# The second column correction is made directly behind its sums, and VectorE adds it to x tile 4

## The reference, cut to what matters

```
def fake_quant(x, s, z):
    q = clip(round(x / s + z), 0, 255)
    return (q - z) * s

x = x + fake_quant(layernorm(x), s1, z1) @ fake_quant(ctx, s2, z2)

y = layernorm(x)
logits = y @ gate_w.T                     # 8 experts, top 2, softmax over the two
x = x + y @ base_w.T + base_b + 2 * sum_e w_e * (y @ A_e.T) @ B_e.T     # rank 16 each
```

## Time and profile before

| what | value |
|---|---|
| median of 3 runs | 197.53 us (196.81 to 198.03) |
| the profiled execution's own time | 196.73 us |
| its span, first to last instruction | 194.9 us |
| mean granted TensorE clock | 0.982 |
| PE busy | 170.9 us (88%) |
| DVE busy | 123.3 us (63%) |
| ACT busy | 77.6 us (40%) |
| POOL busy | 16.2 us (8%) |

### The profile page before, as it was taken

How to read it: one execution, slowest core, us unless ns; L and a number is a source line. 1 busy time by engine, 2 the same in 40 slices (tenths; PEclk the granted TensorE clock), 3 DMA queues, 4 the chain that set the end, 5 groups by cost and what they waited for, 6 DMA issues and landing times.

```text
span 194.9 us, 2441 instructions
## 1 busy us (share of the span) xinstructions
PE 170.9 (88%) x862; PEld 123.3 (63%) x862; DVE 123.3 (63%) x314; ACT 77.6 (40%) x132; POOL 16.2 (8%) x33
## 2 busy tenths in 40 slices
PE   5837687959898998997888399999999999999993
PEld 2312243548686877885376276878688868888882
DVE  0688566889989969899403856765675506561521
ACT  2366949809247152756550412732243230110000
POOL 2022003201010000000041100110011000100000
PEclk9996999999999999999999789999999999999999
DMA  4999996999947520322019590425053500350112
GB/s 90 403 415 409 412 408 256 199 243 347 308 182 152 174 87 20 120 100 108 0 27 182 114 219 0 94 49 148 35 100 58 166 3 0 53 162 0 59 54 105
DMA packets 9515, 29.55 MB, mean 152 GB/s; under 512 B 1184, under 2 KB 1184, under 8 KB 9504
## 3 DMA queue, kind: packets, MB, share of 16 engines
q1 hardware_dynamic: 7344, 22.06, 30.3%
q0 software_dynamic: 2016, 7.34, 20.3%
q10 hardware_dynamic: 144, 0.00, 0.0%
HBM read 22.05 MB, written 4.19 MB: 135 GB/s over the span
## 4 chain that ended last, share of the span: by engine, by line
PE 56%; DVE 23%; ACT 10%; DMA 5%; issue 5%; SPq 0%; DVEq 0%; ACTq 0%
PE ps_odd L837 17%; PE ps_even L837 16%; PE ps_att L795 6%; PE ps_g L829 3%; PE ps_t L779 3%; DMA x_sb<-zfix 2%; DMA x_sb<-in_x 2%; DVE stats L515 2%; DVE x_sb L568 2%; DVE yt L593 2%; DVE stats L511 2%; DVE c L557 2%; ACT zfix L365 1%; DVE w_lo L599 1%; ACT qx L337 1%
## 5 line engine op out<-in xcount | busy, mean ns | idle before, releaser
L837 PE MATMUL ps_even<-w_hi,yt 128*128 128x512 f32 x128 | 38.0, 403 | 0.8 <-ACT zfix L365 0.8
L837 PE MATMUL ps_odd<-w_hi,yt 128*128 128x512 f32 x128 | 36.7, 400 | 0.0
L837 PEld LDWEIGHTS ps_even<-w_hi,yt 128*128 128x128 f32 x128 | 23.7, 192 | 5.6 <-issue 1.0
L795 PE MATMUL ps_att<-c,c1t 128*128 128x512 f16 x96 | 23.9, 389 | 2.3 <-ACT c1t L344 2.3
L837 PEld LDWEIGHTS ps_odd<-w_hi,yt 128*128 128x128 f32 x128 | 22.8, 188 | 4.2
L385 ACT ACTIVATE yt<-ps_t 128x512 fp32r<-128x512 f32 x15 | 9.0, 597 | 33.2 <-PE ps_t L779 33.2
L837 PE MATMUL ps_even<-w_lo,yt 128*128 128x512 f32 x64 | 20.9, 403 | 0.0
L593 DVE TENSOR_TENSOR yt<-ps_t,yt 128x512 fp32r<-128x512 f32 x15 | 10.4, 690 | 15.1 <-ACT yt L385 14.9
L319 ACT ACTIVATE ln_v<-mv,eps 128x1 f32<-128x1 f32 x16 | 4.7, 293 | 37.8 <-DVE mv L516 37.8
L829 PE MATMUL ps_g<-ag,yt 128*128 128x272 f32 x64 | 17.2, 343 | 2.1 <-DVE yt L593 2.1
L837 PE MATMUL ps_odd<-w_lo,yt 128*128 128x512 f32 x64 | 18.7, 392 | 0.0
(11 more groups left out here) (99 smaller groups left out, 252.8 us busy)
## 6 DMA issues: line engine op xcount, KB each, us to landing
ring<-in_ctx SPq DMA_DIRECT2D x12, 512.0 KB, 10.1
w_raw<-in_w_t SPq DMA_DIRECT2D x8, 512.0 KB, 15.5
x_sb<-in_base_b POOLq DMA_DIRECT2D x8, 512.0 KB, 5.4
out_x<-x_sb SPq DMA_DIRECT2D x16, 256.0 KB, 2.5
x_sb<-in_x SPq DMA_DIRECT2D x7, 512.0 KB, 6.5
x_sb<-zfix POOLq DMA_DIRECT2D x6, 512.0 KB, 5.4
x_sb<-in_ctx SPq DMA_DIRECT2D x4, 512.0 KB, 7.9
ag_raw<-in_ag_t SPq DMA_DIRECT2D x1, 544.0 KB, 14.1
```

The source lines that it names most:

```text
L795: ins = pe.matmul(att_bank(t)[h][:, :], c1t[:, t % 4, k, :], c2[:, k, h * HALF:(h + 1) * HALF], start=(k == 0), stop=(k == CT - 1))
L837: pe.matmul(ffn_bank[t % 2][h][:, :], rows_of(part, t, k), w[:, k, h * HALF:(h + 1) * HALF], start=start, stop=False)
```

## The change: what it does

ScalarE makes the second column correction ahead of `scale_x(5)`, and so ahead of the row corrections of tiles 2 and 3 as well. GpSimd no longer issues the DMA that adds it to x tile 4. A new VectorE step `add_zfix_early` adds it, between the constants of tile 5 and `cut_x(5)`, once both halves of `zfix` and the quantisation of tile 4 are there. `add_attention(4)` waits for a semaphore of that step in place of the DMA's. Tiles 5, 6 and 7 still get the correction by DMA. On GpSimd the bias of tile 3 now stands directly behind the bias of tile 2.

```diff
-        zfix_added = {t: sem(f"zfix_added{t}") for t in range(2, TILES)}
+        zfix_added = {t: sem(f"zfix_added{t}") for t in range(2, TILES) if t != TPB}
+        x4_fixed = sem("x4_fixed")
...
@@ GpSimd
             for t in range(TPB, TILES):
-                add_zfix(t)
+                if t > TPB:
+                    add_zfix(t)
                 add_bias(t - 1)
             add_bias(TILES - 1)
@@ ScalarE
             first_guess(0, 5)
+            zero_point_columns(1)
             scale_x(5)
             zero_point_row(2)
             zero_point_row(3)
-            zero_point_columns(1)
@@ VectorE, in add_attention
                 if t == 0:
                     dve.wait_ge(ss_ready, 1)
+                elif t == TPB:
+                    dve.wait_ge(x4_fixed, 1)
                 elif t > 1:
                     dve.wait_ge(zfix_added[t], 16)
@@ VectorE
+            def add_zfix_early():
+                dve.wait_ge(zfix_ready, 4)
+                dve.wait_ge(qx_ready[TPB], 1)
+                dve.tensor_tensor(x_sb[:, TPB, :], x_sb[:, TPB, :], zfix[:, :], ALU.add).then_inc(x4_fixed, 1)
...
             sum_context(7)
             x_constants(5)
+            add_zfix_early()
             cut_x(5)
```

## The result

The changed kernel takes 189.84 us (median of 4 runs, 189.57 to 191.78). The ratio to the kernel before is 0.9636, with a 95% interval of 0.9548 to 0.9723. It is faster, by about the 3.5% that were forecast (190.7 us, range 189.2 to 193.0). The ratio compares the fast executions alone (without one of the kernel before at 200.22 us), so it is not the quotient of the medians. The profiled execution took 189.90 us with a span of 188.1 and a mean granted clock of 0.991; before it was 194.9 and 0.982, so 6.8 us of span are gone, against 6.63 in the sum.

A forecast was written before the change was run, and what follows sets the result against it. TensorE, busy 88%, bounds the kernel, with waits of 4.1 us for y and 0.8 us for zfix. Removing 5.16 us of standing still and 1.47 us of slow clock gives 190.1 us profiled; forecast 190.7 us, range 189.2 to 193.0.

The forecast's parts named there:

- the sum: Block 3 on TensorE shrinks from 25.95 to 19.32 us, a gain of 6.63 us that reaches the end.
- The path: Tile 4's chain into block 3: correction, its addition, attention, y and transposition all come earlier, y ready at 102.8.
- The stop: TensorE's standing still in block 3, waiting for zfix and y of tile 4, goes: 5.16 us.
- The margin of 2.6 us for y: Tile 4's y is ready at 102.8, 2.6 us before TensorE comes to its transposition at 105.46.
- The clock: Behind the wait for y, TensorE's stretch at half clock goes: 1.47 us.
- What was to cost nothing: Work moved on ScalarE, VectorE and the earlier bias transfer loses nothing; covers of 1.1, 0.3 and 4.7 us.
- The shared port: GpSimd's bias issue beside busy VectorE costs 0, upper bound 0.86 us; the skill's rule suggests up to half a microsecond.
- The first: Rival: TensorE's clock falls all the same, in block 3 or later, losing 1.47 us again: 192.2 us; chance 0.08.
- The second rival: ScalarE's or VectorE's order, or the bias, makes tile 4's y or something behind it late: some 194 us; chance 0.08.
- the third and fourth: Rivals: earlier bias delays the last context slab, 200 us; TensorE's 4.1 us wait has another cause, 196.7 us; 0.03 each.
- The step from the profiled execution to the median: Whole-kernel time: the median before lay 0.8 us above its profiled execution, which would turn 190.1 into 190.9 us.

The follow-up runs named there:

- the late-y kernels: The changed kernel with VectorE making y of tile 4 three, five or eight times more before reporting it: 189.83, 191.50 and 195.38 us.
- the kernel with eight repetitions: The changed kernel with VectorE making y of tile 4 eight times more before reporting it: 195.38 us, ratio 0.9896.
- The kernel with five: The changed kernel with VectorE making y of tile 4 five times more before reporting it: 191.50 us, ratio 0.9747.
- The bias held back: The changed kernel with GpSimd holding the bias of tile 3 until both halves of the correction are there: 189.97 us, ratio 0.9611.
- the first alone: The kernel before with only ScalarE's second correction moved ahead of scale_x(5), the DMA still adding it to tile 4: 191.65 us, ratio 0.9675.

## Why the prediction was right

- **The path.** It was read off the chain: zfix, DMA, attention, y, transposition. The changed kernel runs each step within 0.3 us of the time that the sum gave it (zfix done at 95.4 for 95.6, the attention at 97.44 for 97.6, y ready at 102.6 for 102.8, TensorE there at 105.3 for 105.5). Most of that is one offset of 0.16 us, by which this execution was ahead at TensorE's gate matmuls.
- **The stop.** 5.16 us of standing still were to go, and went: block 3 has no wait. The margin of 2.6 us for y is 2.74 in the trace; the late-y kernels put its edge between 2.55 us (nothing lost) and 4.25 us (1.8 lost).
- **The clock.** The 1.47 us are shown by the kernel with eight repetitions: 5.7 us of loss for a stop of 4.2. The kernel with five shows that a stop of 1.7 us cost only itself in the profiled execution; one of its four executions had a mean clock of 0.973 (193.72 us), and where that one lost is not known.
- **What was to cost nothing.** ScalarE's L321 waited for VectorE (1.16 us, forecast 1.1). VectorE's `cut_x(5)` ended at 97.02, 0.4 us before the attention. The last context slab landed 3.5 us after its issue, no later than the 4.5 of the earlier trace rows, beside the bias transfer, which took 7.0 us itself. The bias held back gave 0.0 us.
- **The shared port.** I took 0 for the bias issue beside VectorE, with an upper bound of 0.86 us, and quoted the Trainium skill ("SBUF — State Buffer", section "SBUF: two separate sides") for up to half a microsecond. The rows show 0.04: the cut of the slab began at 80.64, inside the issue of 80.28 to 81.19, and did not wait for its end. By the Trainium skill's rule it should have; the measurement decides, and here an issue that lasts 0.91 us in the profile did not keep the cut waiting for more than 0.04 us. For how long the issue holds the port isn't shown.
- **The rivals.** The first (the clock falls all the same) had 0.08. Its mechanism is real, but it sits elsewhere: behind stops of 2.1 us at 25 and 46 us, in the one traced execution of the lower level. That the kernel before does the same fits its mean clocks (0.957 to 0.974 in 26 of 33 executions), but no trace shows it. Two of 11 executions of the changed kernel were on the lower level, with 191.78 and 192.47 us. I had argued against it that no other stop was followed by a fall, which was true of the one execution that I could see and not of the program. The second rival's shortage (margins of 1.1 and 0.3 us) did not come; the third and fourth are ruled out by the landing of the slab and by the missing wait.
- **The step from the profiled execution to the median.** This term was mis-sized. The sum gave 190.1 us for the profiled execution, which took 189.90; up to 0.8 us was added because the median before lay that much above its profiled execution. Here the median (189.84) lies at the profiled execution. The kernel before was profiled on its upper level, on which it had 7 of 33 executions, and the changed kernel has 9 of 11 on its own. Of the 0.9 us by which the forecast is too high, 0.6 are this step; the other 0.2 or 0.3 are the distance of 190.1 from the times measured, and lie ahead of block 3.
- **The other half microsecond.** On the upper levels the gain is 196.8 - 189.65 = 7.1 us, and 6.63 are traced to block 3. The distance settles where the rest lies: it shrank by 83.24 - 76.63 = 6.61 us, so behind 42 us nothing is left over. Ahead of that point no edit was made, and executions of one program differ there: the changed kernel arrives at 40.97, 41.59 and 41.98 us, in executions in which the clock fell to 0.50 at about 12.4, 13.7 and 14.5 us, around the end (13.1 or 13.2 us) of a stop of TensorE of 2.3 us. The earlier it fell, the more of the slow stretch lay in the stop. The kernel before arrived at 42.16.
- **What stays open.** Why the clock falls in some executions behind stops of 2.1 us and not in others, and where the executions of the lower levels that were not profiled lose their time.

## What to carry to other kernels

Read a wait of the busiest engine together with the clock behind it: here a stop of 4.1 us cost 5.6, and one of 1.7 us cost 1.8. When two edits shorten the same path, measure each alone before keeping both, since here the first alone brought 5.7 of 6.6 us. Compare profiled executions from a fixed point behind the start to a fixed point behind the change: three of one program agree to 0.02 us there, while their spans differ by 1.0 us. Take the price of a gap-free block from a later block of the same form (19.32 us, measured 19.31), and the margin from where the waiting engine would arrive.

## What the runs showed of the hardware that I had not expected

- Two stops of TensorE of 2.1 us were followed by a clock of 0.50 in one profiled execution and not in two others of the same program; the stop of 2.3 us that ends at 13.1 to 13.7 us had a fall to 0.50 in all fourteen traces, between 0.7 us before its end and 1.7 us behind it; the stops of 4.1 and 4.2 us were followed by it in both profiled executions that had one, and the mean clock of seven of eight executions with the 4.2 us stop was 0.982 (the eighth 0.965) where 0.991 was usual without it. None of the 33 executions of the kernel before, which has the stop of 4.1 us, was above 0.983.
- The mean clocks lie on steps: 0.991 and 0.973 for the changed kernel, 0.983, 0.974, 0.965 and 0.957 for the one before, with times from 196.5 to 200.2 us. That a kernel with fewer long stops has fewer steps is not shown: the moved correction alone, with one stop of 0.7 us more than the changed kernel, had 0.964 and 0.970.
- A DMA issue by GpSimd and a VectorE instruction beside it cost each other 0.04 to 0.05 us, at durations of 0.91 and 0.46 us.
